# Perceiver block: the row terms of a quantised product added later, row sums on TensorE, single last context tiles, two PSUM copies on another engine

## What is computed

```python
q1 = clip(round(layernorm(x) / s1 + z1), 0, 255); q2 = clip(round(ctx / s2 + z2), 0, 255)
x = x + ((q1 - z1) * s1) @ ((q2 - z2) * s2)            # quantised product with the context
h = layernorm(x); q = h @ Wq; k, v = split(h @ Wkv)
x = x + attention(q, k, v, causal, distance bias) @ Wo # 32 heads of 64, one k and v
x = x + layernorm(x) @ W + bias                        # W from 4-bit integers, scales, zero points
```

## Time and profile before

| | us |
|---|---|
| median of 3 runs | 397.14 |
| lowest, highest | 396.98, 397.20 |
| the profiled execution | 397.71 |
| its span, first to last instruction | 395.9 |
| TensorE matmuls busy (share of the span) | 354.6 (90%) |
| VectorE busy | 328.7 (83%) |
| ScalarE busy | 221.7 (56%) |
| GpSimd busy | 29.8 (8%) |
| mean granted TensorE clock | 0.981 |
| moved by DMA | 77.37 MB |

### The profile page before, as it was taken

The page is one execution under the profiler, slowest core; times in us unless marked ns, Lnnn a source line. Parts: engine busy times, 40 slices in busy tenths (PEclk is TensorE's granted clock), DMA queues, the critical chain, the costliest instruction groups (busy, mean ns, idle before and its releaser), DMA issues.

```text
span 395.9 us, 5717 instructions
## 1 busy us (share of the span) xinstructions
PE 354.6 (90%) x2342; PEld 265.2 (67%) x2342; DVE 328.7 (83%) x333; ACT 221.7 (56%) x316; POOL 29.8 (8%) x69
## 2 busy tenths in 40 slices
PE   0076865899999999999999999999999999999996
PEld 0022231425888787888877888888888788888884
DVE  1689889797879898884999967888988999999924
ACT  1788988997515872845856570742834923333100
POOL 6000000006590000000011000000000000000000
PEclk9999889699999999999999999999999999999999
DMA  8999999999055487496539624786000020000006
GB/s 333 422 436 424 428 434 427 427 397 395 17 212 170 152 208 218 118 216 208 206 111 269 208 99 165 260 309 223 2 0 1 2 106 2 0 0 2 0 0 212
DMA packets 21958, 77.37 MB, mean 195 GB/s; under 512 B 1354, under 2 KB 1402, under 8 KB 18810
## 3 DMA queue, kind: packets, MB, share of 16 engines
q1 hardware_dynamic: 21924, 77.01, 53.5%
q10 hardware_dynamic: 8, 0.00, 0.0%
HBM read 74.91 MB, written 2.10 MB: 194 GB/s over the span
## 4 chain that ended last, share of the span: by engine, by line
PE 72%; DVE 19%; DMA 4%; issue 3%; ACT 1%; ACTq 0%; DVEq 0%
PE bank L1189 22%; PE bank L1049 11%; PE bank L1050 11%; PE bank L1051 11%; DVE q L708 7%; PE bank L1010 4%; DMA raw<-in_L_attn_Wq 3%; PE bank L1062 2%; DVE stats L622 2%; PE bank L1042 2%; PE bank L1134 2%; DMA prm_row<-in_L_xattn_x_zp 2%; PE bank L1072 1%; PE bank L1153 1%; DVE resid L720 1%
## 5 line engine op out<-in xcount | busy, mean ns | idle before, releaser
L486 ACT ACTIVATE w_hi<-raw 128x2048 fp32r<-128x2048 f32 x29 | 55.2, 1912 | 44.3 <-DMA raw<-in_L_attn_Wo 22.6
L652 DVE TENSOR_TENSOR w_lo<-raw,w_hi 128x2048 fp32r<-128x2048 f32 x27 | 62.6, 2326 | 12.7 <-ACT w_hi L486 12.7
L1189 PE MATMUL bank<-w_hi,hd 128*128 128x512 f32 x208 | 53.2, 391 | 0.1
L1010 PE MATMUL bank<-q,at 128*128 128x512 bf16 x128 | 38.4, 429 | 16.1 <-DVE q L708 15.5
L1189 PEld LDWEIGHTS bank<-w_hi,hd 128*128 128x128 f32 x208 | 38.8, 188 | 8.5 <-issue 0.5
L708 DVE TENSOR_SCALAR q<-q 128x2048 bf16<-128x2048 uint8 x32 | 38.4, 1218 | 4.7 <-PE bank L1017 4.3
L1049 PE MATMUL bank<-w_hi,hd 128*128 128x512 f32 x104 | 40.7, 391 | 0.0
L1050 PE MATMUL bank<-w_lo,hd 128*128 128x512 f32 x104 | 40.5, 389 | 0.0
L1051 PE MATMUL bank<-w_hi,hd 128*128 128x512 f32 x104 | 40.5, 389 | 0.0
L1049 PE MATMUL bank<-w_hi,xt 128*128 128x512 f32 x96 | 38.9, 405 | 0.0
L1050 PE MATMUL bank<-w_lo,xt 128*128 128x512 f32 x96 | 37.5, 390 | 0.0
(11 more groups left out here) (158 smaller groups left out, 616.7 us busy)
## 6 DMA issues: line engine op xcount, KB each, us to landing
raw<-in_ctx SPq DMA_DIRECT2D x8, 2048.0 KB, 15.3
raw<-in_L_attn_Wq SPq DMA_DIRECT2D x16, 1024.0 KB, 6.0
ctx_more<-in_ctx SPq DMA_DIRECT2D x7, 2048.0 KB, 16.1
raw<-in_L_attn_Wo SPq DMA_DIRECT2D x13, 1024.0 KB, 5.1
raw_fifth<-in_L_attn_Wo SPq DMA_DIRECT2D x3, 1024.0 KB, 5.1
resid<-in_x SPq DMA_DIRECT2D x2, 1024.0 KB, 12.6
ctx_more<-in_ctx SPq DMA_DIRECT2D x2, 1024.0 KB, 15.3
scale<-in_L_ffn_scales SPq DMA_DIRECT2D x16, 128.0 KB, 6.7
```

Source lines behind the costliest of these rows:

```text
L486: nc.scalar.activation(hi_slots[s], raw_slots[s], ACT.Copy).then_inc(w_hi_set, 1)
L652: nc.vector.tensor_tensor(lo_slots[s], raw_slots[s], hi_slots[s].bitcast(F32), ALU.subtract).then_inc(w_lo_set, 1)
L1010: mm(bank[:, 4 * b + n, :], at[:, k, b * P:(b + 1) * P], q16[:, i % 2, n * CH:(n + 1) * CH], start=start, stop=False)
L1189: return mm(bank[:, 4 * b + n, :], left[:, j, b * P:(b + 1) * P], right[slot_of(W_F + j)][:, n * CH:(n + 1) * CH], start=part == 0 and j = ...
```

## The change

- The row sums no longer come from VectorE's accumulation in the shift. TensorE forms them with 32 matmuls of one column, all of one bank, after tile 27 (`row_sums`), with `at` as the stationary operand and ones as the moving one.
- The row term is not added to x ahead of the first residual. VectorE works it out for both batches at once behind the last conversion (`row_terms`), and the second residual adds it, as the scalar of a scalar_tensor_tensor.
- The last eight context tiles are loaded one by one, each with its own semaphore; the last in two halves of 1024 columns, which ScalarE rounds, VectorE converts and TensorE multiplies apart.
- The upper parts of groups 2 and 3 of batch 0's transposes are taken out of PSUM by VectorE (`first_upper`), not by ScalarE.

The core of the diff:

```diff
-            for i in range(CTX_TILES // 2 - 1):
+            for i in range((CTX_TILES - CTX_RING) // 2):
...
-            for e in range(2):
-                i = CTX_TILES - 2 + e
+            for s in range(CTX_RING):
+                i = CTX_TILES - CTX_RING + s
                 sp.wait_ge(ctx_q, i - CTX_RING + 1)
-                sp.dma_start(ctx_slots[i % CTX_RING], ctx_pairs[i // 2, :, e]).then_inc(ctx_last[e], 16)
+                if i < CTX_TILES - 1:
+                    sp.dma_start(ctx_slots[s], ctx_pairs[i // 2, :, i % 2]).then_inc(ctx_last[s], 16)
+                else:
+                    sp.dma_start(ctx_slots[s][:, 0:D // 2], ctx_pairs[i // 2, :, i % 2, 0:D // 2]).then_inc(ctx_last[s], 16)
+                    sp.dma_start(ctx_slots[s][:, D // 2:D], ctx_pairs[i // 2, :, i % 2, D // 2:D]).then_inc(ctx_end, 16)
...
+                if i == CTX_TILES - 1:
+                    for h in range(2):
+                        c = slice(h * D // 2, (h + 1) * D // 2)
+                        if h == 1:
+                            act.wait_ge(ctx_end, 16)
+                        nc.scalar.activation(q8[:, i % Q8, c], ctx_slots[i % CTX_RING][:, c], ACT.Identity,
+                                             bias=prm[:, 3:4], scale=inv[:, 2:3]).then_inc((ctx_q_half, ctx_q)[h], 1)
+                    return
...
             for g in range(2):
                 upper(0, g)
-            round_ctx(KT + 9)
-            for g in range(2, 4):
-                upper(0, g)
-            for i in range(KT + 10, CTX_TILES):
+            for i in range(KT + 9, CTX_TILES):
                 round_ctx(i)
...
+            def first_upper(g):
+
+                dve.wait_ge(tr_done, g + 1)
+                dve.wait_ge(hi_out, g)
+                nc.vector.tensor_copy(xt_hi[:, 4 * g:4 * g + 4, 0:P],
+                                      bank[:, tr_bank(0, g), :].rearrange("p (t m) -> p t m", t=4)).then_inc(hi_out, 1)
...
-                nc.vector.tensor_scalar(a16[:, b, :], a8[:, b, :], -QSHIFT, None, ALU.add, ALU.add,
-                                        accum_out=rowsum[:, b:b + 1]).then_inc(a16_set, 1)
-                dve.wait_ge(a16_set, b + 1)
-
-            def add_row_term(b):
-                link(nc.vector.tensor_scalar(rowterm[:, b:b + 1], rowsum[:, b:b + 1], dif[:, 3:4], kdd[:],
+                nc.vector.tensor_scalar(a16[:, b, :], a8[:, b, :], -QSHIFT, None, ALU.add).then_inc(a16_set, 1)
+
+            def row_terms():
+
+                dve.wait_ge(rowsum_done, 1)
+                link(nc.vector.tensor_scalar(rowterm[:], bank[:, ROWSUM_BANK, 0:B], dif[:, 3:4], kdd[:],
                                              ALU.mult, ALU.add))
-                link(nc.vector.tensor_scalar(rowterm[:, b:b + 1], rowterm[:, b:b + 1], ss[:], None, ALU.mult))
-                link(nc.vector.tensor_scalar(resid[:, b, :], resid[:, b, :], rowterm[:, b:b + 1], None, ALU.add))
+                nc.vector.tensor_scalar(rowterm[:], rowterm[:], ss[:], None, ALU.mult).then_inc(rowterm_set, 1)
...
             for g in range(4):
+                if g >= 2:
+                    first_upper(g)
                 remainder(0, g)
                 convert_ctx(KT + 6 + g)
             for i in range(KT + 10, CTX_TILES):
                 convert_ctx(i)
+            row_terms()
             colsums(1)
...
-                nc.vector.tensor_tensor(resid[:, b, c], bank[:, O_BANK[n][b], :], resid[:, b, c],
-                                        ALU.add).then_inc(resid2, 1)
+                if n == 0:
+                    dve.wait_ge(rowterm_set, 1)
+                nc.vector.scalar_tensor_tensor(out=resid[:, b, c], in0=bank[:, O_BANK[n][b], :],
+                                               scalar=rowterm[:, b:b + 1], in1=resid[:, b, c], op0=ALU.add,
+                                               op1=ALU.add).then_inc(resid2, 1)
...
+                if i == CTX_TILES - 1:
+                    pe.wait_ge(ctx_c_half, 1)
+                else:
+                    pe.wait_ge(ctx_c, i + 1)
                 for n in range(NCH):
+                    if i == CTX_TILES - 1 and n == NCH // 2:
+                        pe.wait_ge(ctx_c, i + 1)
                     mm(bank[:, 4 * b + n, :], at[:, k, b * P:(b + 1) * P], q16[:, i % 2, n * CH:(n + 1) * CH],
...
+            def row_sums():
+
+                pe.wait_ge(lo_out, 3)
+                for b in range(B):
+                    for k in range(KT):
+                        ins = mm(bank[:, ROWSUM_BANK, b:b + 1], at[:, k, b * P:(b + 1) * P], ones16[:, 0:1],
+                                 start=k == 0, stop=k == KT - 1)
+                ins.then_inc(rowsum_done, 1)
...
                     if n == 1 and t == 0:
+                        pe.wait_ge(rowterm_set, 1)
...
                 ctx_tile(1, k)
+                if k == 11:
+                    row_sums()
```

More of the change, by code:

```diff
@@ L189, in perceiver @@
         ctx_loaded = [sem(f"ctx_loaded{s}") for s in range(CTX_RING // 2)]
-        ctx_last = [sem(f"ctx_last{e}") for e in range(2)]
+        ctx_last = [sem(f"ctx_last{s}") for s in range(CTX_RING)]
+        ctx_end = sem("ctx_end")
+        ctx_q_half = sem("ctx_q_half")
+        ctx_c_half = sem("ctx_c_half")
         w_loaded = [sem(f"w_loaded{s}") for s in range(RING + 1)]
@@ L217, in perceiver @@
         colsum_out = sem("colsum_out")
+        rowsum_done = sem("rowsum_done")
+        rowterm_set = sem("rowterm_set")
         ctx_done = sem("ctx_done")
@@ L270, in perceiver @@
         AT_BANK = 6
+        ROWSUM_BANK = 2
         Q_BANK = ((0, 1), (2, 3), (0, 1), (2, 3))
@@ L455, in round_ctx @@
             def round_ctx(i):
-                if i < CTX_TILES - 2:
+                if i < CTX_TILES - CTX_RING:
                     act.wait_ge(ctx_loaded[i // 2 % len(ctx_pair_slots)], 16 * (i // CTX_RING + 1))
                 else:
-                    act.wait_ge(ctx_last[i % 2], 16)
+                    act.wait_ge(ctx_last[i % CTX_RING], 16)
                 if i >= Q8:
                     act.wait_ge(ctx_c, i - Q8 + 1)
+                if i == CTX_TILES - 1:
[6 more added lines that the diff above has]
+                    return
                 nc.scalar.activation(q8[:, i % Q8], ctx_slots[i % CTX_RING], ACT.Identity, bias=prm[:, 3:4],
@@ L704, in convert_ctx @@
             def convert_ctx(i):
+                if i == CTX_TILES - 1:
+                    dve.wait_ge(ctx_mm, i - 1)
+                    for h in range(2):
+                        c = slice(h * D // 2, (h + 1) * D // 2)
+                        if h == 0:
+                            dve.wait_ge(ctx_q_half, 1)
+                        else:
+                            dve.wait_ge(ctx_q, i + 1)
+                        nc.vector.tensor_scalar(q16[:, i % 2, c], q8[:, i % Q8, c], -QSHIFT, None,
+                                                ALU.add).then_inc((ctx_c_half, ctx_c)[h], 1)
+                    return
                 dve.wait_ge(ctx_q, i + 1)
@@ L745, in _ @@
             convert_ctx(13)
-            add_row_term(1)
             convert_ctx(14)
@@ L1007, in ctx_tile @@
                 start, stop = k == 0, k == KT - 1
-                pe.wait_ge(ctx_c, i + 1)
+                if i == CTX_TILES - 1:
+                    pe.wait_ge(ctx_c_half, 1)
+                else:
+                    pe.wait_ge(ctx_c, i + 1)
                 for n in range(NCH):
+                    if i == CTX_TILES - 1 and n == NCH // 2:
+                        pe.wait_ge(ctx_c, i + 1)
                     mm(bank[:, 4 * b + n, :], at[:, k, b * P:(b + 1) * P], q16[:, i % 2, n * CH:(n + 1) * CH],
```

2 lines of the change are left out of this document (removed).

## The result

| | before | changed |
|---|---|---|
| median of 5 runs, us | 397.14 | 405.62 |
| the runs, us | 396.87 to 397.20 | 400.73, 402.15, 405.62, 409.72, 410.17 |
| the profiled execution, us | 397.71 | 410.17 |
| its span | 395.9 | 408.3 |
| its mean granted TensorE clock | 0.981 | 0.958 |

The changed kernel is slower in every run, by 0.9% to 3.3%. The forecast was 399.3, with a range of 397.0 to 401.4. Before, the five runs lie within 0.33 us; now they spread over 9.4. That spread was the first sign that something other than a sum of durations was at work.

A forecast was written before the change was run, and what follows sets the result against it. The bound was TensorE's release by the context stage (93.89 us), set by VectorE, then its alternation with TensorE, plus a fixed 302 us. Terms -0.6 + 1.6 - 0.3 + 1.45 = +2.15 gave a median of 399.3 us, range 397.0 to 401.4.

The forecast's parts named there:

- just inside: End of the context stage: ScalarE finishes tile 31 at 90.99, slightly before the alternation of VectorE and TensorE, the claimed bound.
- Row terms, -0.6: Before batch 0's transposes: less VectorE work puts tile 19 out of the way, so conversion 22 starts 0.6 us earlier.
- Row sums, +1.6: Behind tile 27 on TensorE: 32 uncovered one-column matmuls with their loads, taken at 50 ns each, add 1.6 us.
- rival of loads end to end: Row sums behind tile 27: 32 loads of 105 ns take 3.4 us instead of 1.6, giving 401.1 us; chance 0.10.
- Alternation, -0.3: Last four context tiles: VectorE gets two tiles ahead during the row sums, so they go at 1.30 instead of 1.39; -0.3 us.
- Two uppers, +1.45: VectorE between 77.67 and 85.4: two casts of 0.69 each plus short waits, in a stretch without gaps, add 1.45 us.
- Queued behind them are conversions 24 to 31, and TensorE behind those: Behind VectorE's two added casts: the later conversions and TensorE's work move later with the casts' +1.45 us.
- the two zeros: Around tile 31: row-term steps lie in VectorE's 1.48 us wait, and halves gain nothing while TensorE does tile 30; 0 each.
- The first one: Tiles 19, 20 and batch 0's transposes: clock stays up (-2.15 instead of -0.6), sums are cheap; 396.6 us, chance 0.12.
- a sign of being wrong: Batch 0's transposes: TensorE running at 2.4 GHz through them would show the forecast wrong.
- The clock falls again: Behind the row sums: TensorE drops to the half level, adding 1.6 us for 400.9 us; chance 0.13.
- With halves ... 0.: Tile 31: its matmuls could start half a conversion earlier, but TensorE is busy with tile 30 until then; 0.

The follow-up runs named there:

- row sums alone: The 32 one-column matmuls behind tile 27 added to the kernel before, sums unused; 397.15 us, ratio 1.0004.
- small step from PSUM: The kernel before with one more 128x2 VectorE step, source in PSUM and result unused, between batch 1's two column-sum operations; 397.35 us, ratio 1.0004.
- the first three experiments: Changed kernel, separately: GpSimd starting only behind conversion 31, 402.62 us; half conversions accumulating into an unread tile, 400.73; tile 31 in one piece, 401.29 to 406.68.
- the one-step kernel: Changed kernel with the row terms in one step from PSUM, factors multiplied with ss at the start; six runs, 397.74 to 409.81 us.
- the third experiment: Changed kernel with tile 31 in one piece for load, rounding, conversion and matmuls; four runs, 401.29 to 406.68 us, ratio 1.014.
- the two uppers alone: The kernel before with only batch 0's two upper parts moved to VectorE; four runs: 398.42, 404.99, 405.00, 406.48 us.
- the one with early row sums: Changed kernel with row sums behind tile 15 in bank 5, row terms behind batch 0's column sums; eight runs 396.79 to 398.36 us, three 409.45 to 409.81.
- the best kernel: Changed kernel with row sums behind tile 15, row terms behind batch 0's column sums, and the two upper parts back on ScalarE; 396.72 us, ratio 0.999.
- the first experiment: Changed kernel with GpSimd starting its two subtractions only when VectorE has converted tile 31; 402.62 us, ratio 1.0132.

## Why the prediction was wrong

- **What bounds the kernel.** The reading was right on that: what happens behind 94 us is a fixed length, and 12.7 us lost ahead of it were 12.46 of the whole. That ScalarE ends "just inside" holds for the one profile that I had. In two others of the same order up to tile 27 (row sums alone, small step from PSUM) ScalarE releases conversion 31.
- **Up to tile 27 it has to be told twice.** The profiled execution of the changed kernel had TensorE's low stretches at other places than the one that I started from. Four other profiles have the same order of work up to tile 31 (the first three experiments and the one-step kernel), and in them the forecast is met nearly to the tenth.
- **Row terms, -0.6.** In those four the batch-0 chain waits for ScalarE's square root, the normalising ends at 72.4 to 72.6, the transposes run at the half clock, and conversion 22 starts at 77.0 to 77.2 (forecast 77.07). In the changed kernel's own profile the normalising started at 72.09, not earlier: tile 22's DMA came 0.3 us later, and TensorE ran 60.5 to 70.5 us at the half clock (a mean of 0.51, before 1.00 from 60 to 68), so the batch-0 chain was not ahead. What came back there was the faster clock from 71 us on (twelve transposes in 1.62 instead of 2.82): conversion 22 at 76.43 instead of 77.67, -1.24.
- **Row sums, +1.6.** Mis-sized. They take 0.82 us, 26 ns each, nearer the lower bound (16 ns) than the 50 that I chose. Each of the 32 loads lasts 96 ns, but they start every 26, so a load's duration was no bound. That decides against the rival of loads end to end and its 3.4 us.
- **Alternation, -0.3.** From conversion 27 to conversion 31 the four profiles have 6.10 us, before 5.55: the 0.82 of the sums less 0.27. In the changed kernel's profile it was 6.37.
- **Two uppers, +1.45.** Right as a duration, 0.68 and 0.69. In the four, conversion 27 starts at 86.55 to 86.72 (forecast 86.6). In the changed kernel's profile it came at 87.23, 1.48 later than before, with -1.24 ahead of it and a wait of 1.49 us for a tile 25 that ran at the half clock (84.67).
- **The sum.** With 0.82 for the row sums it gives +1.37 for conversion 31. The four have 1.35 to 1.52. The changed kernel's profile has 2.30, and that this is close to my +2.15 is chance: a clock that fell once more, and a term twice too large. Only one run shows the time without a collision, the lowest of the one-step kernel: 397.74, 0.6 above the kernel before. It was not profiled, and why it is not 1.4 stays open.
- **The step that failed** is the one on what is queued behind the casts ("Queued behind them are conversions 24 to 31, and TensorE behind those"), with the two zeros beside it, for the row-term steps and for the halves. I moved conversion 31 later microsecond by microsecond and took its duration, and that of the steps, from rows where GpSimd stood still. I had looked at who waits for the conversion, not at who runs beside it. In the profiled execution 2.3 us of lateness carried it to 93.60, behind GpSimd's start (93.19, before 92.95); 1.5 were enough for the second half in the one-step kernel. From there on: 4.94 + 4.99 instead of 0.65 + 0.65, 8.6 us; then TensorE, starved, at the half clock from 98.5 to 108, which makes eight matmuls 3.68 instead of 2.12 us:

```profile
98.50:103.00 4.50, 1.04 (x2) 0.13 (x2) 4.50 (x2) 1.91 (x1) 4.40 (x1) 0.50 0.26 109
103.00:108.00 5.00, 4.49 (x13) 2.65 (x14) 2.31 (x5) 0.00 (x0) 0.00 (x0) 0.50 0.00 0
```

- **"With halves ... 0."** Two instructions instead of one made it worse: one conversion can be caught by one subtraction, two by two. The eight runs of delayed kernels with tile 31 whole (the third experiment and the two uppers alone) have no time near 410; with halves there are such times in the changed kernel (two of five), in the one with the one-step row terms (one of six) and in the one with early row sums (three of eleven). The counts are small; the profiles are what shows it.
- **Rivals.** The first one's two conditions both came: the transposes of batch 0 ran at the full clock, which I had also named as a sign of being wrong, and the sums cost under 1.0 us. Its gain did not: -1.24 instead of -2.15, and all of it lost again at tile 25. In the four other profiles the transposes had the half clock, as I had forecast. "The clock falls again" did happen, but behind the starvation and not behind the row sums. None of my rivals named a collision of two engines that exchange nothing.

## What to carry to other kernels

A duration from a trace holds for the neighbours that it had. Before moving work later, look at every engine beside its new place, also those without a semaphore between them; here 0.42 us of distance between a VectorE conversion and a GpSimd subtraction was worth 4.3 us an instruction. The distance can be kept by moving small work into earlier gaps, and the risk taken away by a source in PSUM or another form of the instruction. A kernel whose runs spread over several separate values after a change may have such a threshold, and then a single good run says nothing. And a profile is one execution: here which engine was the last bound changed from one profile to the next.

## What the runs showed that I had not expected

- GpSimd's subtraction holds VectorE out up to its own end whatever VectorE's size: 4.24 to 4.51 us for 128x2 numbers (0.23 alone), 5.57 for 128x2048 (1.22 alone); 3.09 and 2.26 when the small step came in the middle. In the other order GpSimd took 5.54 instead of 4.64.
- What was not held, beside GpSimd at work: the accumulating conversion (1.22), a step or cast from PSUM (0.28, 0.69), statistics (0.69), an operation with one input in PSUM and one in SBUF (0.75), and steps on 128x1 numbers with one input (0.15 and 0.17 at 100.97 and 101.29 in the best kernel). A tensor_scalar on 128x2 was held, the one on 128x1 was not; the step on 128x1 with two inputs in SBUF was (0.46).
- Full-array matmuls of one column, each with a new 128x128 bf16 load, start every 26 ns at full clock.
- The same code runs with TensorE's low stretches at other places from one execution to the next. The changed kernel and the first experiment have the same order up to GpSimd's start; the clock fell at 50.4, 60.7 and 84.6 us in the profile of the one, at 59.2 and 72.8 in that of the other. Tile 25 in the first and in the second:

```profile
84.67 1.89 PE L1050 MATMUL bank<-q,at 128*128 128x512 bf16 x4 [1.09 <-DVE q L739]
```

```profile
85.13 1.04 PE L1052 MATMUL bank<-q,at 128*128 128x512 bf16 x4 [1.09 <-DVE q L741]
```

The first half of conversion 31 then starts at 93.60 in the first and at 92.72 in the second; with GpSimd starting between 92.84 and 93.20 in the four profiles of this order in which nothing holds it back, that is the difference between both halves caught and at most the second. GpSimd's own start moves too, by up to 0.4 us. That it is the clock that decides from run to run fits the five profiles, but was not tested by itself. The kernel before hides all this: all its runs on record lie within 1.3 us.
